# Feed-forward of layer 0: bias rows written into the product banks by ScalarE instead of added by bias matmuls

## The chip, the cores and the metric

The kernel runs on one core of a Trainium2 chip. The metric is device time in microseconds (us), the median of several runs. The engines are named as in the profile: PE is TensorE (PEld its weight loads), ACT is ScalarE, DVE is VectorE, POOL is GpSimd, SP is SyncE. SP here only issues DMAs. A name with a q behind it (PEq, SPq) is an engine's instruction queue.

## What is computed

Two decoder layers in one launch, on 2048 tokens of width 512: attention 0, feed-forward 0, attention 1, feed-forward 1. The change lies in feed-forward 0, of which the reference says (x is the residual stream; the constant names are cut):

```python
def _quant_dequant_fp8(x):                 # per row, per chunk of 128
    scale = maximum(amax(chunk), 1e-4) / 448
    return (chunk / scale).astype(float8_e4m3fn) * scale
D = Xd @ W0d.T + bias0                     # 512 -> 1792
D = gelu(D, approximate=False)
Dd = quant_dequant(D.astype(bfloat16))
E = Dd @ W1d.T + bias1                     # 1792 -> 512
x = x + E.astype(bfloat16)
```

Xd, W0d and W1d are the layer-normed input and the two weights after the same quantisation. The biases bias0 (1792 values) and bias1 (512) are bfloat16.

## The kernel before

Each stage is one function with one block of instructions per engine; a block begins when every engine has ended the one before. `ffn0` works through 16 tiles of 128 tokens. Operands of the products are split into a high and a low float16 part, and a product is the sum of three passes (high by high, high by low, low by high). Products are scaled by 64 (`WEIGHT_SCALE`), and ScalarE divides by 64 where it reads a bank.

**One tile.** The input is quantised (ACT L1083, DVE `quant_x`, POOL L1277), transposed by PE into the bank `xt` (L1035), and split into XD by ACT (`high_x`, L1124) and DVE (`low_x`, L1206). The first product fills four banks `db0` to `db3`, 448 of the 1792 columns each: one bias matmul (L1026) and twelve of the product (L1028). Gelu (ACT L1113) reads each bank into DB. DVE takes the maxima (`amax_d`, L1184), works out scales in fifteen small steps (`scales_d`, L70 to L85), ACT multiplies by the reciprocals (L1093, 14 pieces), DVE rounds to the grid (`grid_d`, L100 to L107, and `off_grid_d`, L1202), ACT multiplies by the scales (L1100), and ACT and DVE split into HL (`high_d`, L1108; `low_d`, L1214). SP transposes HL into DT by DMA (L1005, L1007). The second product goes into the one bank `eb`: one bias matmul (L1041, 512 columns), then 42 of the product (L1045). ACT reads it (`out_e`, L1120) and POOL adds it to X (L1282).

**The bias matmul.** Its stationary operand `ones` is 128 by 128, zero but for a first row of ones; its moving operand `B0S` or `B1S` has the scaled bias in row 0 and zeros in the others. It is the first matmul of each accumulation group (start=True), so it also opens the bank. To have this, SP loads bias0 and bias1 into one partition (L995, L996), POOL clears B0S, B1S and `ones` and sets the row (L1292 to L1295), and DVE scales the biases (`scale_biases`, L1226) in step -1. PE waits for both before its first product (L1057 to L1060).

**Order.** All engines but SP go through the steps -1 to 18 (`steps`, L983); tiles 6 to 13 run in a hardware loop of two tiles a turn. In step i PE does the first product of tile i, the transposes of tile i+1, and the second product of tile i-2 (L1055). ACT does in this order: `out_e` of tile i-3, L1083 for tile i+2, gelu of the first three banks of tile i, the first half of L1100 for tile i-1, gelu of the fourth bank, `high_x` of tile i+1, `high_d` and the second half of L1100 and `high_d` for tile i-1, L1093 for tile i (L1132). DVE: `grid_d` of tile i-1, `quant_x` of i+2, `off_grid_d` of i-1, `amax_d` of i, `low_x` of i+1, `scales_d` of i, `low_d` of i-1 (L1228). So gelu of tile i waits on ACT behind work that itself waits for DVE, and DVE starts tile i's grid only after ACT has done the first seven pieces of L1093. In steps 0 to 4 DVE also has a piece each of the layer norm and scales of the last quarter of X.

**End of the stage.** In step 15 SP loads the key and value weights of attention 1 (L337), and ACT and DVE split them (L1147, L1245). In steps 16 and 17 PE projects keys and values with them into the same banks `db` (L348). Behind step 16 ACT and DVE do two parts of the next layer norm (L189 is ACT's square root in it), so `out_e` of tile 14 stands on ACT behind them, and PE's second product of tile 15 waits for `out_e` of tile 14, since there is one bank `eb`. The memory `SH` that holds the biases becomes the query weights WQ1 in step 17 (L1166).

The weights W0T of the first product are loaded during attention 0 (L748); W1T is loaded by SP behind the biases (L997), on the same queue.

Of the kernel before, what the change touches and what calls it, by code (L numbers as in the profile page):

```python
# [16 lines left out]
BF16 = mybir.dt.bfloat16  # L17
# [6 lines left out]
P = 128  # L24
# [898 lines left out]
def ffn0(nc, sb, pb, sem, X, ident, ahead_of_ffn0, x_scales, x_buffers, x_sems, w1t_dram, b0, b1,  # L923
# [4 lines left out]
    with ExitStack() as ph:  # L928
# [8 lines left out]
        B0, B1, B0S = SH[0:1, 0:INNER], SH[0:1, INNER:INNER + DIM], SH[:, INNER + DIM:2 * INNER + DIM]  # L937
        B1S = sb(ph, "B1S", [P, DIM], BF16)
        ones = sb(ph, "ones0", [P, P], BF16)
# [15 lines left out]
                 "xt_done xt_hi xt_lo d_done ones_done bias_zeroed bias_ready gelu_done da_done dstep dw_done dcut dbits dm_done dsum "  # L955
# [37 lines left out]
        @block.sync  # L993
        def _(sp):
            sp.dma_start(B0[:, :], b0.partition_broadcast(1)).then_inc(S["b_ld"], 16)  # L995
            sp.dma_start(B1[:, :], b1.partition_broadcast(1)).then_inc(S["b_ld"], 16)  # L996
            sp.dma_start(W1T[:, :, :, :], w1t_dram.rearrange("p (s c n) -> p s c n", s=2, c=IC)).then_inc(S["w1_ld"], 16)  # L997

            def step(i):
                hidden = ahead(i, -1)  # L1000
                if live(hidden):
                    if live(ahead(hidden, -1)):
                        sp.wait_ge(S["e_done"], count(hidden, 1, 0))
                    sp.wait_ge(S["dh_done"], count(hidden, 2, 2))
                    sp.dma_start_transpose(DT[:, 0, :, :], HL[:, 0, :, :].rearrange("p c t -> p (c t)")).then_inc(S["dt_done"], 16)  # L1005
                    sp.wait_ge(S["dl_done"], count(hidden, 2, 2))
                    sp.dma_start_transpose(DT[:, 1, :, :], HL[:, 1, :, :].rearrange("p c t -> p (c t)")).then_inc(S["dt_done"], 16)  # L1007

            for i in range(TILES + 1):
                if i == TILES - 1:  # L1010
                    sp.wait_ge(S["xqs_done"], TILES)
                    load_kv1(sp)
                if i == TILES:
                    sp.wait_ge(S["d_done"], 4 * TILES)
                    load_weights1(sp)
                step((0, i))

        @block.tensor
        def _(pe):
            def first_product(i, qs):  # L1020
                for q in qs:
                    if q == 0:
                        pe.wait_ge(S["xt_lo"], count(i, 1, 1))
                    if live(ahead(i, -1)):
                        pe.wait_ge(S["gelu_done"], count(i, 4, q - 3))
                    pe.matmul(db[q][:, 0:NQ], ones[:, :], B0S[:, q * NQ:(q + 1) * NQ], start=True, stop=False)  # L1026
                    for n, (k, (a, b)) in enumerate([(k, ab) for ab in PASSES for k in range(KC)]):
                        last = pe.matmul(db[q][:, 0:NQ], XD[:, i[1] % 2, a, k, :], W0T[:, b, k, q * NQ:(q + 1) * NQ],  # L1028
                                         start=False, stop=n == 3 * KC - 1)
                    last.then_inc(S["d_done"], 1)  # L1030
# [7 lines left out]
            def second_product(i):  # L1038
                if live(ahead(i, -1)):
                    pe.wait_ge(S["eb_done"], count(i, 1, 0))  # L1040
                pe.matmul(eb[:, :], ones[:, :], B1S[:, :], start=True, stop=False)  # L1041
                pe.wait_ge(S["dt_done"], count(i, 32, 32))
                for c in range(IC):
                    for a, b in PASSES:
                        last = pe.matmul(eb[:, :], DT[:, a, c, :], W1T[:, b, c, :],  # L1045
                                         start=False, stop=c == IC - 1 and (a, b) == PASSES[-1])
# [8 lines left out]
            def step(i):  # L1055
                old, nxt = ahead(i, -2), ahead(i, 1)
                if fixed(i) == 0:  # L1057
                    pe.wait_ge(w0_ld, 16)
                    pe.wait_ge(S["ones_done"], 2)
                    pe.wait_ge(S["bias_ready"], 2)  # L1060
# [15 lines left out]
        def _(act):  # L1076
# [38 lines left out]

            def out_e(i):
# [3 lines left out]
                act.activation(EB[:, i[1] % 2, :], eb[:, :], ACT.Copy, scale=UNSCALE).then_inc(S["eb_done"], 1)  # L1120

# [10 lines left out]
            def step(i):  # L1132
# [5 lines left out]
                if fixed(i) == -1:  # L1138
                    high_x(nxt)
# [4 lines left out]
                if fixed(i) == TILES - 1:  # L1144
                    act.wait_ge(loaded1["skv_ld"], 32)
                    act.wait_ge(S["xt_done"], TILES)
                    act.activation(WKV1[:, 0, :, :, :], SKV1[:, :, :, :], ACT.Copy, scale=WEIGHT_SCALE).then_inc(S["kvw_hi"], 1)  # L1147
                if live(hidden):
# [3 lines left out]
                if live(nxt) and fixed(i) != -1:  # L1152
                    high_x(nxt)
                if live(hidden):
# [7 lines left out]
                if fixed(i) == TILES + 1:  # L1162
                    high_keys_values((2, 3))
                    act.wait_ge(loaded1["sq_ld"], 16)
                    for j in range(REP):
# [7 lines left out]
        def _(dve):  # L1173
# [48 lines left out]
            def scale_biases():  # L1222
                dve.wait_ge(S["b_ld"], 32)
                dve.wait_ge(S["bias_zeroed"], 2)
                for scaled, bias in ((B0S, B0), (B1S, B1)):
                    dve.tensor_scalar(scaled[0:1, :], bias[:, :], WEIGHT_SCALE, None, ALU.mult).then_inc(S["bias_ready"], 1)  # L1226

            def step(i):  # L1228
                hidden, nxt, after = (ahead(i, by) for by in (-1, 1, 2))
                if fixed(i) == -1:  # L1230
                    low_x(nxt)
                    scale_biases()
# [39 lines left out]
        def _(pool):  # L1272
# [17 lines left out]

            for zeros in (B0S, B1S):
                pool.memset(zeros[:, :], 0.0).then_inc(S["bias_zeroed"], 1)  # L1292
            pool.memset(ones[:, :], 0.0).then_inc(S["ones_done"], 1)
            pool.wait_ge(S["ones_done"], 1)
            pool.memset(ones[0:1, :], 1.0).then_inc(S["ones_done"], 1)  # L1295
# [746 lines left out]
```

## Time and profile before

| | |
|---|---|
| runs | 1663.59, 1663.84, 1664.19 us; median 1663.84 |
| profiled execution, first to last instruction | 1663.4 us |
| busy share of that span | PE 91%, DVE 77%, ACT 47%, POOL 17% |
| mean granted TensorE clock | 0.968 |
| feed-forward 0 | from 1023.7 to 1380.8 us of the span |

The page gives the span of the profiled execution and no other time for it; the runs shown are 0.2 to 0.8 us longer. All times of rows are us from the start of that span. A matmul's duration in a row reaches until its results are out, so consecutive matmuls overlap: what one costs is the distance between starts, not its duration. Some matmul records are missing in a trace: L1041 shows its 16 weight loads and no matmuls. "Idle before" in a row is the time in which that engine did nothing just before, and the name behind the arrow is what released it.

### The profile page before, as it was taken

The numbers are of one execution on the slowest core, as the hardware profiler recorded it, in microseconds if no ns is written. First come the engines' busy times: TensorE is split into PE (matmuls) and PEld (weight loads), VectorE is DVE, ScalarE is ACT, GpSimd is POOL, SyncE is SP. The second block draws the span as 40 slices with busy tenths as digits, with TensorE's granted clock in tenths as the row PEclk, the third lists the DMA queues.
The fourth block names the chain that finished last, engine by engine and source line by source line (L and its number), as shares of the span: only waits on it lengthen the run. The fifth ranks groups of instructions, "written<-read, shape, count | busy, mean of one in ns | idle before, by whom it ended". The sixth has DMA issues, their size and how long they took to land. (4 is left out here: it accounts for less than half of the span.)

```text
span 1663.4 us, 29998 instructions
## 1 busy us (share of the span) xinstructions
PE 1510.4 (91%) x11382; PEld 803.7 (48%) x11398; DVE 1273.3 (77%) x2386; ACT 789.3 (47%) x1677; POOL 289.0 (17%) x249
## 2 busy tenths in 40 slices
PE   5799999999999999999999987799999998787695
PEld 4455455555555555555555543344444544344353
DVE  6577667667677667767776786899999986999777
ACT  3343433424334243342333332566777763888652
POOL 2001002001011011011011001111211103789620
PEclk7799999999999999999999998899999999899898
DMA  7031231321312212221312112122222350767402
GB/s 265 1 78 51 68 85 26 79 75 43 98 39 66 76 52 64 68 61 52 77 51 62 48 70 102 23 45 45 45 44 44 58 117 1 140 107 123 79 1 101
DMA packets 273838, 113.48 MB, mean 68 GB/s; under 512 B 239154, under 2 KB 255539, under 8 KB 273460
## 3 DMA queue, kind: packets, MB, share of 16 engines
q1 hardware_dynamic: 234820, 78.67, 21.6%
q10 hardware_dynamic: 38896, 33.03, 6.3%
q8 instruction: 94, 1.54, 0.4%
q14 instruction: 28, 0.23, 0.0%
HBM read 44.57 MB, written 11.53 MB: 34 GB/s over the span
## 5 line engine op out<-in xcount | busy, mean ns | idle before, releaser
L627 PE MATMUL xp<-WO,OT 128*128 128x512 f16 x1536 | 341.1, 382 | 5.6 <-DVE X L824 5.6
L585 PE MATMUL pj<-XT,WQ 128*128 128x512 f16 x1536 | 339.0, 381 | 6.4 <-PEq L379 6.4
L627 PEld LDWEIGHTS xp<-WO,OT 128*128 128x128 f16 x1536 | 148.2, 98 | 189.3 <-issue 18.4
L585 PEld LDWEIGHTS pj<-XT,WQ 128*128 128x128 f16 x1536 | 148.4, 98 | 182.3 <-DVE WKV L294 6.7
L705 ACT ACTIVATE E<-E 128x512 f32<-128x512 f32 x64 | 40.1, 627 | 329.0 <-DVE E L801 329.0
L824 DVE SCALAR_TENSOR_TENSOR X<-xp,X 128x512 f32<-128x512 f32 x128 | 88.2, 690 | 113.0 <-PE xp L627 112.0
L565 POOL TENSOR_TENSOR VW<-VW,XB 128x1024 f32<-128x1024 f32 x14 | 32.9, 2351 | 769.8 <-DVE VW L107 769.8
L1028 PE MATMUL db<-W0T,XD 128*128 128x448 f16 x768 | 162.2, 363 | 0.0
L1045 PE MATMUL eb<-W1T,DT 128*128 128x512 f16 x672 | 147.7, 380 | 4.2 <-ACT EB L1120 2.5
L766 DVE SCALAR_TENSOR_TENSOR QT<-pj,QT 128x512 f16<-128x512 f32 x128 | 88.0, 687 | 67.9 <-ACT QT L688 67.6
L1028 PEld LDWEIGHTS db<-W0T,XD 128*128 128x128 f16 x768 | 76.9, 100 | 74.7 <-issue 8.0
L688 ACT ACTIVATE QT<-pj 128x512 f16<-128x512 f32 x128 | 75.5, 590 | 71.1 <-PE pj L585 71.0
L1100 ACT ACTIVATE VD<-VD,dscale 128x128 f32<-128x128 f32 x224 | 68.7, 390 | 75.1 <-DVE VD L1202 75.1
L1045 PEld LDWEIGHTS eb<-W1T,DT 128*128 128x128 f16 x672 | 65.6, 98 | 78.7 <-DMA DT<-HL 1.1
L775 DVE TENSOR_TENSOR OT<-tv,OT 128x512 f16<-128x512 f32 x128 | 82.3, 684 | 13.8 <-ACT OT L697 11.1
L590 PE MATMUL pj<-WKV,CT 128*128 128x128 f16 x1536 | 91.3, 220 | 0.9 <-DVE QT L766 0.9
L585 PE MATMUL pj<-CT,WKV 128*128 128x512 f16 x384 | 88.2, 380 | 4.0 <-DVE QT L766 4.0
L590 PEld LDWEIGHTS pj<-WKV,CT 128*128 128x128 f16 x1536 | 85.9, 98 | 7.7 <-issue 6.3
L697 ACT ACTIVATE OT<-tv 128x512 f16<-128x512 f32 x128 | 69.3, 593 | 26.2 <-PE tv L616 26.2
L710 ACT ACTIVATE EH<-E 128x512 f16<-128x512 f32 x64 | 40.3, 630 | 84.5 <-DVE E L813 84.5
L1401 POOL TENSOR_TENSOR CT<-CT 128x512 f16<-128x512 f32 x64 | 72.6, 1159 | 16.9 <-ACT CT L1631 16.7
L1093 ACT ACTIVATE VD<-DB,drec 128x128 f32<-128x128 bf16 x224 | 67.2, 387 | 12.3 <-DVE drec L85 12.3
(236 smaller groups left out, 2427.0 us busy)
## 6 DMA issues: line engine op xcount, KB each, us to landing
W0T<-in_L_xattn_wq ACTq DMA_DIRECT2D x7, 1024.0 KB, 5.3
W0T<-in_L_xattn_wo ACTq DMA_DIRECT2D x7, 1024.0 KB, 5.0
CS<-in_ctx SPq DMA_DIRECT2D x4, 1024.0 KB, 10.1
X<-in_x SPq DMA_DIRECT2D x4, 1024.0 KB, 11.2
out<-X SPq DMA_DIRECT2D x8, 512.0 KB, 3.6
XB<-in_L_ffn_W ACTq DMA_DIRECT2D x28, 128.0 KB, 2.8
w0t<-XB ACTq DMA_DIRECT2D x7, 512.0 KB, 3.3
w1t<-W0T ACTq DMA_DIRECT2D x7, 512.0 KB, 3.8
```

The lines of the kernel that those rows point to most:

```text
L585: last = pe.matmul(bank[:, :], w, src[:, b, k, tokens], start=n == 0, stop=n == 3 * KC - 1)
L590: last = pe.matmul(bank[:, i * P:(i + 1) * P], CT[:, a, k, own], WKV[:, b, k, 1, :], start=n == 0, stop=n == 3 * KC - 1)
L627: last = pe.matmul(xp[i % 2][:, :], OT[:, a, j, i * P:(i + 1) * P], WO[:, b, j, :], start=n == 0, stop=n == 3 * REP - 1)
L688: act.activation(QT[:, 0, :, u, :], q_bank(u), ACT.Copy, scale=UNSCALE).then_inc(S["pj_hi"], 1)
L697: act.activation(o_out(0, pair, h), o_bank(h), ACT.Copy).then_inc(S["ot_hi"], 1)
L766: dve.scalar_tensor_tensor(out=to[0], in0=q_bank(u), scalar=UNSCALE, in1=to[1], op0=ALU.mult, op1=ALU.subtract).then_inc(S["pj_lo"], 1)
L775: dve.tensor_tensor(o_out(1, pair, h), o_bank(h), o_out(0, pair, h), ALU.subtract).then_inc(S["ot_lo"], 1)
L824: dve.scalar_tensor_tensor(out=xt, in0=xp[i % 2][:, :], scalar=UNSCALE, in1=xt, op0=ALU.mult, op1=ALU.add).then_inc(S["x_acc"], 1)
L1028: last = pe.matmul(db[q][:, 0:NQ], XD[:, i[1] % 2, a, k, :], W0T[:, b, k, q * NQ:(q + 1) * NQ], start=False, stop=n == 3 * KC - 1)
L1045: last = pe.matmul(eb[:, :], DT[:, a, c, :], W1T[:, b, c, :], start=False, stop=c == IC - 1 and (a, b) == PASSES[-1])
L1100: last = act.activation(VD[:, r, c, :], VD[:, r, c, :], ACT.Copy, scale=ds_[:, r, c:c + 1])
L1401: pool.tensor_tensor(EH[:, 1, q, :], E[:, q, :, :].rearrange("p u n -> p (u n)"), EH[:, 0, q, :], ALU.subtract).then_inc(S["e_lo"], 1)
```

## The change

The biases are loaded into all 128 partitions. `ones`, B0S, B1S, POOL's four memsets and DVE's `scale_biases` are gone. In step -1 PE opens each of the five banks once with a matmul whose result nobody reads (`open_banks`), now ahead of the first transposes, and ACT then writes the scaled biases into all five banks, ahead of `high_x` and L1083. From then on all product matmuls have start=False and add to what stands in the bank, and ACT writes the bias anew after each read: into `db0` to `db2` behind the three gelus of a step (for the next tile), into `db3` behind `high_x`, into `eb` behind `out_e`. PE waits for these writes (`bias_set`, `e_bias_set`) where it waited for gelu and `out_e`. ACT waits for its own gelu or `out_e` ahead of the write into the bank that this read, and ahead of L1166 for all its writes.

```diff
-        B0, B1, B0S = SH[0:1, 0:INNER], SH[0:1, INNER:INNER + DIM], SH[:, INNER + DIM:2 * INNER + DIM]
-        B1S = sb(ph, "B1S", [P, DIM], BF16)
-        ones = sb(ph, "ones0", [P, P], BF16)
+        B0, B1 = SH[:, 0:INNER], SH[:, INNER:INNER + DIM]
@@ block.sync
-            sp.dma_start(B0[:, :], b0.partition_broadcast(1)).then_inc(S["b_ld"], 16)
-            sp.dma_start(B1[:, :], b1.partition_broadcast(1)).then_inc(S["b_ld"], 16)
+            sp.dma_start(B0[:, :], b0.partition_broadcast(P)).then_inc(S["b_ld"], 16)
+            sp.dma_start(B1[:, :], b1.partition_broadcast(P)).then_inc(S["b_ld"], 16)
@@ block.tensor
+            def open_banks():
+                for q in range(4):
+                    pe.matmul(db[q][:, 0:NQ], W0T[:, 0, 0, 0:P], W0T[:, 0, 0, 0:NQ], start=True, stop=True).then_inc(S["opened"], 1)
+                pe.matmul(eb[:, :], W0T[:, 0, 0, 0:P], W0T[:, 0, 0, 0:DIM], start=True, stop=True).then_inc(S["opened"], 1)
             def first_product(i, qs):
...
-                    if live(ahead(i, -1)):
-                        pe.wait_ge(S["gelu_done"], count(i, 4, q - 3))
-                    pe.matmul(db[q][:, 0:NQ], ones[:, :], B0S[:, q * NQ:(q + 1) * NQ], start=True, stop=False)
+                    pe.wait_ge(S["bias_set"], count(i, 4, q + 1))
...
             def second_product(i):
-                if live(ahead(i, -1)):
-                    pe.wait_ge(S["eb_done"], count(i, 1, 0))
-                pe.matmul(eb[:, :], ones[:, :], B1S[:, :], start=True, stop=False)
+                pe.wait_ge(S["e_bias_set"], count(i, 1, 1))
                 pe.wait_ge(S["dt_done"], count(i, 32, 32))
...
-                if fixed(i) == 0:
+                if fixed(i) == -1:
                     pe.wait_ge(w0_ld, 16)
-                    pe.wait_ge(S["ones_done"], 2)
-                    pe.wait_ge(S["bias_ready"], 2)
+                    open_banks()
@@ block.scalar
+            def preset_d(qs):
+                for q in qs:
+                    act.activation(db[q][:, 0:NQ], B0[:, q * NQ:(q + 1) * NQ], ACT.Copy, scale=WEIGHT_SCALE).then_inc(S["bias_set"], 1)
+            def preset_after_gelu(i, qs):
+                act.wait_ge(S["gelu_done"], count(i, 4, qs[-1] + 1))
+                preset_d(qs)
+            def preset_e():
+                act.activation(eb[:, :], B1[:, :], ACT.Copy, scale=WEIGHT_SCALE).then_inc(S["e_bias_set"], 1)
             def out_e(i):
...
+                if live(ahead(i, 1)):
+                    act.wait_ge(S["eb_done"], count(i, 1, 1))
+                    preset_e()
...
                 if fixed(i) == -1:
+                    act.wait_ge(S["b_ld"], 32)
+                    act.wait_ge(S["opened"], 5)
+                    preset_d(range(4))
+                    preset_e()
                     high_x(nxt)
                 if live(after):
                     x_times_rec(after)
                 if live(i):
                     gelu(i, (0, 1, 2))
...
+                if live(nxt) and live(i):
+                    preset_after_gelu(i, (0, 1, 2))
                 if live(hidden):
                     d_times_scale(hidden, 0)
                 if live(i):
                     gelu(i, (3,))
                 if live(nxt) and fixed(i) != -1:
                     high_x(nxt)
+                if live(nxt) and live(i):
+                    preset_after_gelu(i, (3,))
...
                     act.wait_ge(loaded1["sq_ld"], 16)
+                    act.wait_ge(S["bias_set"], 4 * TILES)
+                    act.wait_ge(S["e_bias_set"], TILES)
@@ block.vector
-            def scale_biases():
...
@@ block.gpsimd
-            for zeros in (B0S, B1S):
-                pool.memset(zeros[:, :], 0.0).then_inc(S["bias_zeroed"], 1)
-            pool.memset(ones[:, :], 0.0).then_inc(S["ones_done"], 1)
-            pool.wait_ge(S["ones_done"], 1)
-            pool.memset(ones[0:1, :], 1.0).then_inc(S["ones_done"], 1)
```

## Rows read from the trace of the kernel before

**Rows 1.** Busy time by stretch: stretch, length, PE, PEld, DVE, ACT, POOL, PEclk, DMA, GB/s.
```profile
1170.00:1326.00 156.00, 155.58 (x784) 77.82 (x790) 146.71 (x283) 112.94 (x320) 26.94 (x15) 1.00 0.26 47
```
**Rows 2.** Timeline of one tile's turn: start, us, what, [idle before <-releaser].
```profile
1187.29 0.68 DVE L1206 TENSOR_TENSOR XD<-xt,XD 128x512 f16<-128x512 f32 x1
...
1189.87 0.35 PE L1026 MATMUL db<-SH,ones 128*128 128x448 bf16 x1
...
1191.07 4.20 ACT L1093 ACTIVATE VD<-DB,drec 128x128 f32<-128x128 bf16 x14 [0.51 <-DVE drec L85]
...
1192.33 0.35 PE L1026 MATMUL db<-SH,ones 128*128 128x448 bf16 x1
...
1193.25 0.63 DVE L100 TENSOR_SCALAR VD<-VD 128x896 uint32<-128x896 uint32 x1 [0.22 <-ACT VD L1093]
...
1200.36 9.23 PE L1045 MATMUL eb<-W1T,DT 128*128 128x512 f16 x42
...
1209.43 0.35 PE L1026 MATMUL db<-SH,ones 128*128 128x448 bf16 x1
...
1212.76 0.63 DVE L100 TENSOR_SCALAR VD<-VD 128x896 uint32<-128x896 uint32 x1 [0.20 <-ACT VD L1093]
```
**Rows 3.** Waits from 1165 to 1330: who for whom, us in total, times, longest.
```profile
ACT VD L1100 <- DVE VD L1202: 35.9, 8, 4.8
ACT VD L1093 <- DVE drec L85: 4.9, 9, 0.7
...
DVE VD L100 <- ACT VD L1093: 1.9, 9, 0.2
```
**Rows 4.** Timeline: three gelus in a row on ACT.
```profile
1196.82 1.38 ACT L1113 ACTIVATE DB<-db 128x448 bf16<-128x448 f32 x3
```
**Rows 5.** Groups by line: four copies out of SBUF; last columns busy us, mean ns, idle.
```profile
L1166 ACT ACTIVATE SH<-W0T 128x512 f16<-128x512 f32 x4 | 2.2, 637 | 0.0
```
**Rows 6.** Timeline of the start of feed-forward 0.
```profile
1023.68 0.30 SPq L995 DMA_DIRECT2D SH<-in_L_ffn_bias  x1
...
1024.38 0.60 ACT L1124 ACTIVATE XD<-xt 128x512 f16<-128x512 f32 x1 [13.92 <-PE xt L1035]
...
1025.01 0.69 DVE L1206 TENSOR_TENSOR XD<-xt,XD 128x512 f16<-128x512 f32 x1 [1.63 <-ACT XD L1124]
...
1025.83 0.61 DVE L1226 TENSOR_SCALAR SH<-SH 1x1792 bf16<-1x1792 bf16 x1
...
1027.23 0.53 PE L1026 MATMUL db<-SH,ones 128*128 128x448 bf16 x1 [2.88 <-POOL ones L1295]
...
1031.34 0.35 PE L1026 MATMUL db<-SH,ones 128*128 128x448 bf16 x1
```
**Rows 7.** DMA issues of the whole span: size, median us from issue to landing.
```profile
w0t<-XB ACTq DMA_DIRECT2D x7, 512.0 KB, 3.3
...
W0T<-in_L_ffn_bias SPq DMA_DIRECT2D x1, 256.0 KB, 6.8
```
**Rows 8.** Waits of SP's queue from 1300 to 1385: us in total, times, longest.
```profile
SPq L1005 <- PE eb L1045: 6.3, 3, 2.8
```
**Rows 9.** Timeline of the end of feed-forward 0.
```profile
1335.71 1.06 ACT L1147 ACTIVATE VW<-VW 128x1024 f16<-128x1024 f32 x1 [0.84 <-DMA VW<-in_L_xattn_Wv]
...
1339.27 1.09 DVE L1184 TENSOR_REDUCE damax<-DB 128x7 f32<-128x896 bf16 x1 [0.70 <-ACT DB L1113]
...
1368.35 0.21 ACT L189 ACTIVATE root<-var_eps 128x4 f32<-128x4 f32 x1 [4.10 <-DVE var_eps L159]
1368.47 0.58 ACT L1120 ACTIVATE EB<-eb 128x512 bf16<-128x512 f32 x1
...
1369.33 9.23 PE L1045 MATMUL eb<-W1T,DT 128*128 128x512 f16 x42 [2.51 <-ACT EB L1120]
```
**Rows 10.** Timeline: two first matmuls of a tile after idle time of PE.
```profile
1061.03 0.56 PE L1026 MATMUL db<-SH,ones 128*128 128x448 bf16 x1 [9.35 <-DVE XD L1206]
...
1126.97 0.36 PE L1026 MATMUL db<-SH,ones 128*128 128x448 bf16 x1 [1.10 <-DVE XD L1206]
```

More of the change, by code:

```diff
@@ L954, in ffn0 @@
         names = ("w1_ld b_ld kvw_hi kvw_lo qw_hi "
-                 "xt_done xt_hi xt_lo d_done ones_done bias_zeroed bias_ready gelu_done da_done dstep dw_done dcut dbits dm_done dsum "
+                 "xt_done xt_hi xt_lo d_done opened bias_set e_bias_set gelu_done da_done dstep dw_done dcut dbits dm_done dsum "
                  "dq_done dqs_done dh_done dl_done dt_done e_done eb_done x_done")
@@ L1023, in first_product @@
                         pe.wait_ge(S["xt_lo"], count(i, 1, 1))
-                    if live(ahead(i, -1)):
-                        pe.wait_ge(S["gelu_done"], count(i, 4, q - 3))
-                    pe.matmul(db[q][:, 0:NQ], ones[:, :], B0S[:, q * NQ:(q + 1) * NQ], start=True, stop=False)
+                    pe.wait_ge(S["bias_set"], count(i, 4, q + 1))
                     for n, (k, (a, b)) in enumerate([(k, ab) for ab in PASSES for k in range(KC)]):
                         last = pe.matmul(db[q][:, 0:NQ], XD[:, i[1] % 2, a, k, :], W0T[:, b, k, q * NQ:(q + 1) * NQ],
-                                         start=False, stop=n == 3 * KC - 1)
+                                         start=False, stop=n == 3 * KC - 1, skip_group_check=True)
                     last.then_inc(S["d_done"], 1)
@@ L1045, in second_product @@
                         last = pe.matmul(eb[:, :], DT[:, a, c, :], W1T[:, b, c, :],
-                                         start=False, stop=c == IC - 1 and (a, b) == PASSES[-1])
+                                         start=False, stop=c == IC - 1 and (a, b) == PASSES[-1], skip_group_check=True)
                 last.then_inc(S["e_done"], 1)
@@ L1220, in low_keys_values @@
                     low_kv1(dve, db[unit], unit // 2, unit % 2)
-            def scale_biases():
[L1223 to L1226, printed above, removed]
             def step(i):
@@ L1231, in step @@
                     low_x(nxt)
-                    scale_biases()
                 if live(hidden):
```

## The prediction

> **What bounds the kernel now.** I read the busy times of the stretch in which feed-forward 0 runs evenly, then the timeline of one tile's turn, then who waits for whom there, and last the two ends of the stage, where the change adds or moves steps.
>
> In the even stretch, eight tiles long, PE is busy for 155.58 of 156.00 us [rows 1]. That looks like a stage bound by PE, and 80 matmuls fewer like a gain. The timeline says otherwise. PE starts a tile every 1209.43 - 1189.87 = 19.56 us, and DVE its grid every 1212.76 - 1193.25 = 19.51 us [rows 2]: two cycles of nearly one length. Which of them drives? `low_x` has XD ready at 1187.97, and PE takes it up 1.90 us later [rows 2], so PE is behind and nobody is held up by it. DVE's own waits in the stretch are 1.9 us in nine grids, all for ACT's L1093, which waits for DVE's `scales_d` [rows 3]: the ring is DVE, ACT, DVE, with no PE in it. DVE's busy share of 146.71 in 156.00 [rows 1] is not slack; what is missing lies between small dependent steps. ACT waits 4.8 us a tile for DVE ahead of L1100, and about half a microsecond ahead of L1093 [rows 3]. The first is room for new work on ACT, the second hardly any.
>
> So a faster PE only starts each tile sooner after `low_x`, and the time changes where PE or ACT stands in a chain: at the start, in the 0.51 us ahead of L1093, and at the end.
>
> **PE's part.** A quarter of the first product is 13 matmuls in 1192.33 - 1189.87 = 2.46 us [rows 2], 0.189 each; one of 512 columns costs (1209.43 - 1200.36) / 42 = 0.216 [rows 2]. A tile loses 4 x 0.189 + 0.216 = 0.97 us, 16 tiles 15.6 us. In the ring this is worth nothing from tile 2 on; DVE's 1.9 us of waits bounds it from above. Tile 0's first product is an exception, below. Its five opening matmuls run while the biases are still coming, and cost nothing as long as that takes longer than they do: about 1 us at 0.2 each, 2 at half the clock.
>
> **The start.** Now PE's first matmul waits until 1027.23 for POOL's `ones`; `high_x` starts at 1024.38 and `low_x` ends at 1025.70, 1.32 later [rows 6]. After the change `high_x` stands behind five writes of ACT, and these behind the biases.
> - Biases: issued at 1023.68; the one-partition loads had landed when DVE scaled them at 1025.83 [rows 6]. Now 448 and 128 KB. The nearest size, 512 KB, lands in 3.3 us; another broadcast bias of 256 KB took 6.8, queued behind other loads [rows 7]. Scaled by size, 3.3 x 576 / 512 = 3.7: landed at 1027.4, between 1025.8 and 1030.5.
> - Five writes: no row has ACT writing a bank. Three gelus of 448 columns take 1.38 us, 0.46 each [rows 4]; four copies of 512 out of SBUF take 2.2 us, 0.55 each, and 0.64 for one alone [rows 5]. A piece of 128 columns takes 4.20 / 14 = 0.30 [rows 2], which a wider one exceeds. I take 0.47 and 0.55, nearest in size: 4 x 0.47 + 0.55 = 2.4, between 1.5 and 3.2.
> - So XD of tile 0 is ready at 1027.4 + 2.4 + 1.3 = 1031.1 and PE starts at 1031.2, 4.0 later than now. Its four bias matmuls are gone, 0.8 less: gelu, and with it DVE's ring, starts **3.2 us later** (0.7 to 7.1 by the bounds). L1083 of tile 1, also behind the writes, has the whole first product of tile 0 as cover.
>
> The Trainium skill, "ScalarE: Activation LUTs", section "The pipeline for one element", says that ScalarE writes PSUM faster than SBUF. No row here shows it; by it the five writes take less than 2.4 us and the start costs less than 3.2.
>
> **The ring.** Per tile ACT gets 4 x 0.47 + 0.55 = 2.4 us. The writes to `db0` to `db2` stand ahead of the 4.8 us wait [rows 3] and vanish in it; `eb`'s delays L1083 and three gelus by 0.6, in the same cover. The write to `db3` stands ahead of `high_d`, L1100 and so L1093: 0.47 against 0.51 of idle [rows 2]: **0 us**. If a write takes its 0.64, 0.13 a tile for some ten tiles: +1.3. Were that idle gone, every tenth on ACT would be a tenth on DVE. The added waits for ACT's own gelus name work that is just ending; behind them queue `high_d` and L1100, counted here.
>
> **The end.** SP's transposes waited for PE three times, up to 2.8 us [rows 8]. Behind one of them stands the key and value load, for which ACT waits 0.84 us; it delays gelu of tile 15, for which DVE waits 0.70 [rows 9]. PE now comes some 2.8 us earlier, this wait goes, and DVE is late by 0.7 less, not more, since ACT's L1100 stands next: -0.7. Then the last second product: `out_e` of tile 14 stands behind the layer norm's square root on ACT (1368.35) and ends at 1369.05; PE's 42 matmuls start at 1369.33 [rows 9]. Now ACT's write of `eb` comes between, 0.6 us, where the bias matmul took 0.28 with its wait: +0.35. Sum **-0.35** (-0.7 to +0.4).
>
> **The clock at the end.** PE has everything else done earlier and waits longer for this last product: 2.51 us now [rows 9], plus 2.8, less 0.35: about 5.0. After 9.35 us of idle time the first matmul took 0.56 us, after 2.88 us 0.53, after 1.10 us 0.36 [rows 6, 10]: the lower clock level twice, the higher once. But at the end 2.51 us cost no clock: 42 matmuls in 9.23, as in the even stretch [rows 2, 9]. 5.0 is beyond both, so I expect the lower level. Its price: the first quarter at the start took 1031.34 - 1027.23 = 4.11 [rows 6] where 2.46 is usual: **+1.65**. Nothing hides it: `out_e`, POOL's add and the next block follow.
>
> **Sum.** 3.2 + 0 - 0.35 + 1.65 = +4.5 us. The profiled span is 1663.4 and the median of the runs 1663.84, 0.4 more; I add the difference to the median: **1668.3 us**. About 0.2%, 3.3 us, is what a measurement of this kernel can tell from no change.
>
> **Rivals.**
> - The clock stays up for the last product (not slower). What decides is whether 5.0 us of idle time lowers it; for it speaks the row with 2.51, against it those with 2.88 and 9.35. Then +2.85, 1666.7: within 0.2%. Chance 0.27.
> - PE was the bound: its 155.58 of 156.00 us speaks for it, the 1.90 us of lag and DVE's few waits against. Then eight tiles gain 0.97 each, 1668.3 - 7.8 = 1660.5. Chance 0.06.
> - A write into a bank costs 0.64 or more and the ring grows: 1669.6. Chance 0.10.
> - The broadcast loads land late, as the 6.8 us row: +3.1, 1671.4. Chance 0.08.
> - The clock falls in every tile, since PE now idles 19.51 - 18.59 = 0.92 us in each. Then a tile's PE time is 18.59 + 1.65 = 20.2, above the ring by 0.7, for nine tiles +6: 1674. The 1.10 us row speaks against. The Trainium skill, "TensorE: Matmul & The Clock Gate", section "HAM oscillation", describes such a repeated loss in a loop with gaps. Chance 0.04, and 0.45 for my forecast.
>
> **Range and chances.** 1664.5 to 1671.5 takes in the forecast, the kept clock, the longer ring and the late load, and leaves out PE as the bound and the clock in every tile. Slower: 0.40 of the forecast's 0.45, and 0.22 of the last three rivals, 0.62. Faster: 0.06. The rest, 0.32, within 0.2%.
>
> **What would show it.** Right: `low_x` of tile 0 ends near 1031; DVE still waits 0.2 us a tile for L1093 with 19.5 us between grids; PE waits about 0.9 us a tile for XD; the last second product takes some 10.9 us. Wrong: a tile's turn near 18.6 (PE was the bound); L1093 no longer waiting for `drec` and the turn longer (ring); the last product in 9.2 (clock); the ring's start moved by under 2 or over 5 us.

## The result and the profile after

The changed kernel takes 1670.53 us (median of 9 runs, 1668.90 to 1671.27); the kernel before, run beside it, 1664.44. The ratio is 1.0029, with an interval of 1.0020 to 1.0039: **slower by 3.3 to 6.5 us**, 4.8 by the ratio and 6.1 by the medians. The forecast was 1668.3, in a range to 1671.5.

The profiled execution has a span of 1669.0 us. Its feed-forward 0 goes from the first issue at 1022.67 to the next block's first matmul at 1386.35, 363.68 us; before it was 1023.68 to 1380.77, 357.09. What follows took 282.65 and 282.63 us. So **all of it, 6.59 us in these two executions, lies in the stage that was changed** (the stage began 1.0 us sooner; over all the profiles below it begins anywhere from 1020.98 to 1023.92).

The even stretch first: busy times by stretch of the kernel after, columns as in [rows 1].

```profile
1170.00:1326.00 156.00, 150.10 (x755) 73.54 (x753) 146.73 (x278) 133.48 (x361) 27.87 (x16) 1.00 0.25 47
```

PE is busy 5.5 us less, ACT 20.5 us more, DVE as before. The clock stays at 1.00. Waits from 1165 to 1330, columns as in [rows 3]:

```profile
ACT VD L1098 <- DVE VD L1224: 23.0, 9, 2.6
...
PE db L1029 <- DVE XD L1228: 5.9, 8, 1.0
DVE VD L100 <- ACT VD L1091: 1.7, 8, 0.2
...
ACT VD L1091 <- DVE drec L85: 0.4, 1, 0.4
```

Two things changed places. PE now waits for XD, 0.7 to 1.0 us a tile, where it was late before. And ACT's slack is used up: ahead of its scaling (L1098, before L1100) it waits 2.6 us a tile instead of 4.8, and ahead of L1091 (before L1093) no longer. The timeline of one tile shows how exactly:

```profile
1187.84 2.16 ACT L1098 ACTIVATE VD<-VD,dscale 128x128 f32<-128x128 f32 x7 [2.63 <-DVE VD L1224]
...
1190.80 0.53 ACT L1116 ACTIVATE db<-SH 128x448 f32<-128x448 bf16 x1
...
1191.56 0.67 DVE L1228 TENSOR_TENSOR XD<-xt,XD 128x512 f16<-128x512 f32 x1
...
1192.37 9.25 PE L1029 MATMUL db<-W0T,XD 128*128 128x448 f16 x48 [1.00 <-DVE XD L1228]
...
1194.34 0.95 ACT L1106 ACTIVATE HL<-VD 128x896 f16<-128x896 f32 x1
...
1195.13 0.17 DVE L85 TENSOR_TENSOR drec<-dtmp 128x14 f32<-128x14 f32 x1
...
1195.34 4.20 ACT L1091 ACTIVATE VD<-DB,drec 128x128 f32<-128x128 bf16 x14
...
1203.16 1.48 ACT L1116 ACTIVATE db<-SH 128x448 f32<-128x448 bf16 x3
...
1211.80 4.52 PE L1029 MATMUL db<-W0T,XD 128*128 128x448 f16 x23 [0.68 <-DVE XD L1228]
```

ACT ends `high_d` at 1195.29 and DVE ends `drec` at 1195.30: they arrive together. The turn is 1211.80 - 1192.37 = 19.43 us; in both kernels turns of 19.43 and 19.51 alternate. The first instruction of DVE's grid for tiles 0, 14 and 15, before and then after:

```profile
1047.02 0.62 DVE L100 TENSOR_SCALAR VD<-VD 128x896 uint32<-128x896 uint32 x1
...
1327.56 0.63 DVE L100 TENSOR_SCALAR VD<-VD 128x896 uint32<-128x896 uint32 x1 [0.22 <-ACT VD L1093]
...
1345.77 0.63 DVE L100 TENSOR_SCALAR VD<-VD 128x896 uint32<-128x896 uint32 x1 [0.22 <-ACT VD L1093]
```

```profile
1051.16 0.62 DVE L100 TENSOR_SCALAR VD<-VD 128x896 uint32<-128x896 uint32 x1
...
1331.83 0.63 DVE L100 TENSOR_SCALAR VD<-VD 128x896 uint32<-128x896 uint32 x1 [0.22 <-ACT VD L1091]
...
1349.25 0.63 DVE L100 TENSOR_SCALAR VD<-VD 128x896 uint32<-128x896 uint32 x1 [0.22 <-ACT VD L1091]
```

From the first grid to that of tile 14 the ring takes 0.13 us more than before, 280.67 and 280.54; from there to the last grid it takes 17.42 and 18.21.

The start, in the timeline (answers to [rows 6]):

```profile
1022.67 0.36 SPq L993 DMA_DIRECT2D SH<-in_L_ffn_bias  x1
1022.71 0.92 PE L1020 MATMUL db<-W0T 128*128 128x448 f16 x4 [1.06 <-PEq L485]
...
1027.69 1.94 ACT L1116 ACTIVATE db<-SH 128x448 f32<-128x448 bf16 x4 [18.00 <-DMA SH<-in_L_ffn_bias]
1029.58 0.58 ACT L1123 ACTIVATE eb<-SH 128x512 f32<-128x512 bf16 x1
1030.10 0.57 ACT L1136 ACTIVATE XD<-xt 128x512 f16<-128x512 f32 x1
...
1031.45 11.57 PE L1029 MATMUL db<-W0T,XD 128*128 128x448 f16 x48 [7.17 <-DVE XD L1228]
...
1042.86 0.60 PE L1036 MATMUL xt<-ident,VW 128*128 128x128 f32 x4
```

The biases land 5.02 us after the first issue, five writes take 2.41, and PE's first product starts 8.78 us after the issue, where it was 3.55. It then takes 42.86 - 31.45 = 11.41 us, at the lower clock level for nearly its first 5; before, it took 11.49 (1027.23 to 1038.72). So DVE's ring starts 5.15 us later, counted from the start of the stage: 28.49 after it, where it was 23.34.

The end (answers to [rows 9]), and the clock in stretches of the last product:

```profile
1371.83 0.20 ACT L189 ACTIVATE root<-var_eps 128x4 f32<-128x4 f32 x1 [4.10 <-DVE var_eps L159]
1371.94 0.58 ACT L1129 ACTIVATE EB<-eb 128x512 bf16<-128x512 f32 x1
...
1372.55 0.60 ACT L1123 ACTIVATE eb<-SH 128x512 f32<-128x512 bf16 x1
...
1373.21 10.93 PE L1044 MATMUL eb<-W1T,DT 128*128 128x512 f16 x42 [3.63 <-ACT eb L1123]
```

```profile
1373.21:1375.00 1.79, 1.79 (x7) 0.77 (x8) 1.72 (x5) 1.79 (x4) 0.54 (x1) 0.75 0.00 0
1375.00:1377.00 2.00, 2.00 (x6) 0.65 (x5) 2.00 (x4) 1.22 (x3) 0.00 (x0) 0.50 0.00 0
```

The last 42 matmuls take 10.93 us instead of 9.23, with the granted clock at 0.50, the 1.2 GHz level, from 1375 to 1377. From the last grid to the start of this product it takes 0.40 us more, and the last grid itself comes 0.79 us sooner behind that of tile 14. **Sum: 5.15 + 0.13 - 0.79 + 0.40 + 1.70 = 6.59**, what the stage is longer.

### The profile page after: what moved, and what is told of

It reads as the page before. It is cut to its first block and busy times, and to the rows that moved or that the text cites. A ratio compares the mean times of both kernels' runs of the same rounds, so it can differ in the third digit from the quotient of the medians.

```text
span 1669.0 us, 29950 instructions
## 1 busy us (share of the span) xinstructions
PE 1499.0 (90%) x11323; PEld 794.2 (48%) x11323; DVE 1272.0 (76%) x2384; ACT 829.4 (50%) x1757; POOL 285.3 (17%) x245
## 5 line engine op out<-in xcount | busy, mean ns | idle before, releaser
L1029 PE MATMUL db<-W0T,XD 128*128 128x448 f16 x768 | 154.6, 363 | 33.9 <-DVE XD L1228 33.9
L1098 ACT ACTIVATE VD<-VD,dscale 128x128 f32<-128x128 f32 x224 | 68.8, 390 | 50.5 <-DVE VD L1224 50.5
L1292 POOL TENSOR_TENSOR VW<-VW,xscale 128x512 f32<-128x512 f32 x15 | 24.3, 1617 | 281.3 <-DVE VW L1200 273.6
```

The source lines that it names most:

```text
L1098: last = act.activation(VD[:, r, c, :], VD[:, r, c, :], ACT.Copy, scale=ds_[:, r, c:c + 1])
```

## The experiments

Each experiment has one profile and 5 to 12 timed runs. "Stage" is as above; "first product" is its start after the start of the stage; the last column is the duration of the last second product. Ratios are against the kernel before, run beside each; its medians there were 1665.20 to 1665.56, so rows are better compared by their ratios than by their medians.

| kernel | median us | ratio (95%) | stage | first product | last product |
|---|---|---|---|---|---|
| before | 1664.44 | | 357.09 | 3.55 | 9.23 |
| after | 1670.53 | 1.0029 (1.0020 to 1.0039) | 363.68 | 8.78 | 10.93 |
| e1_no_bias_matmuls | 1663.99 | 0.9994 (0.9985 to 1.0003) | 357.52 | 3.55 | 10.93 |
| e2_early_biases | 1666.54 | 1.0015 (1.0005 to 1.0025) | 359.54 | 5.03 | 11.07 |
| e3_x_first | 1668.46 | 1.0024 (1.0014 to 1.0035) | 360.54 | 6.02 | 11.06 |
| e4_write_twice | 1674.70 | 1.0056 (1.0042 to 1.0070) | 367.99 | 9.24 | 10.86 |
| e5_keep_busy | 1671.53 | 1.0034 (1.0021 to 1.0047) | 363.54 | 10.50 | 9.24 |
| e6_out_first | 1666.51 | 1.0013 (1.0003 to 1.0023) | 362.54 | 10.91 | 9.22 |
| e7_all | 1660.59 | 0.9975 (0.9966 to 0.9985) | 354.44 | 3.11 | 9.22 |
| e8_before_out_first | 1662.34 | 0.9990 (0.9980 to 0.9999) | 355.29 | 3.55 | 9.24 |
| e9_hold_w1t | 1668.90 | 1.0023 (1.0013 to 1.0033) | 362.37 | 7.45 | 10.93 |
| e10_own_wait | 1668.90 | 1.0024 (1.0015 to 1.0034) | 362.27 | 7.37 | 10.93 |
| e11_hold_and_busy | 1669.67 | 1.0023 (1.0012 to 1.0034) | 361.58 | 7.91 | 9.24 |
| e12_hold_again | 1668.47 | 1.0023 (1.0014 to 1.0033) | 361.40 | 7.48 | 10.83 |

### e1: what PE's 15.6 us are worth

The kernel before without its 80 bias matmuls; the biases are left out of the result, all else (loads, memsets, waits) stays.

```diff
-                    pe.matmul(db[q][:, 0:NQ], ones[:, :], B0S[:, q * NQ:(q + 1) * NQ], start=True, stop=False)
...
-                                          start=False, stop=n == 3 * KC - 1)
+                                          start=n == 0, stop=n == 3 * KC - 1)
...
-                pe.matmul(eb[:, :], ones[:, :], B1S[:, :], start=True, stop=False)
...
```

> The kernel before without its 80 bias matmuls (the first matmul of each product opens the bank); the biases are left out of the result, nothing else changes. Theory (the ring DVE, ACT, DVE sets the pace, PE has slack): 15.6 us less on PE give almost nothing. First product of tile 0 -0.8, end of the stage -0.8 and -0.25, and up to +1.7 if the clock falls ahead of the last product: between -1.9 and +0.2 us against the kernel before, and about 19.5 us between DVE's grids. Rival (PE is the bound of the even stretch): 0.97 us for each of 8 or more tiles, 8 to 15 us faster, about 18.6 us between the grids.

The time is that of the kernel before within its interval, and the stage is 0.43 us longer in the profile. From the first grid to that of tile 14 it takes 280.63 us, before 280.54. Busy times by stretch, and two waits from 1165 to 1330:

```profile
1170.00:1326.00 156.00, 152.43 (x769) 75.14 (x768) 146.77 (x278) 113.20 (x325) 26.96 (x15) 1.00 0.27 50
```

```profile
ACT VD L1091 <- DVE drec L85: 5.0, 9, 0.7
PE db L1027 <- DVE XD L1204: 3.6, 5, 0.8
```

PE gets idle time and gives none of it to the ring: **PE did not bound the stage**. ACT's half microsecond ahead of its L1091 is still there (5.0 us, before 4.9 [rows 3]), so it is the writes that use it up. The last product, after 2.81 us of idle time, took 10.93: the clock can be lost there without any write, by the saving on PE alone.

### e2 and e3: the start

e2 loads the biases during attention 0, into memory that its query weights have left by then. e3 leaves the loads and puts `high_x` and L1081 ahead of the wait for the biases.

```diff
+            sp.wait_ge(S["pj_done"], GROUPS * SPG * 6)
+            sp.dma_start(SH[:, 0:INNER], b0.partition_broadcast(P)).then_inc(bias_ld, 16)
+            sp.dma_start(SH[:, INNER:INNER + DIM], b1.partition_broadcast(P)).then_inc(bias_ld, 16)
```

```diff
                 if fixed(i) == -1:
+                    high_x(nxt)
+                if live(after):
+                    x_times_rec(after)
+                if fixed(i) == -1:
                     act.wait_ge(S["b_ld"], 32)
...
-                    high_x(nxt)
-                if live(after):
-                    x_times_rec(after)
```

> The kernel after, with the biases loaded by SP during attention 0 into the same memory, once the last projection has read it; the order on ACT as in the kernel after. Theory (the first product waits for the biases to land, 5.0 us after their issue, then for five writes): ACT starts to write when the banks are open, some 1.5 us after the block's start instead of 5.0; the first product starts 3.5 us earlier, perhaps 0.5 more by a shorter low clock: 3.5 to 4.2 us faster than the kernel after, about +1 to +2 against the kernel before. Rival (the start is covered by other work, and the loss lies in the ring or at the end): within 0.5 us of the kernel after.

> The kernel after, with high_x and L1081 of step -1 ahead of the wait for the biases and the five writes on ACT. Theory (landing, writes and the split of x stand in one chain): the first product then starts with the first bank's write, 0.5 us after the landing, instead of after five writes, high_x and low_x: 3.2 us earlier, so 3.2 us faster than the kernel after, +1.5 to +2.5 against the kernel before. Rival (landing alone sets the start): no more than 0.5 us faster than the kernel after.

With the loads out of the way the first product starts 3.75 us sooner than in the changed kernel and the stage is 4.14 shorter; with `high_x` first 2.76 and 3.14. Neither reaches the kernel before: the end is as slow as in the changed kernel (11.07 and 11.06). In the timed runs less of the gain shows than the 3.5 to 4.2 and 3.2 us expected: by the ratios e2 is 2.3 us under the changed kernel and e3 0.8, with intervals that overlap the changed kernel's, so for e3 a gain in time is not shown, only the shorter stage.

### e4: is there room for more on ACT?

The write into `db3` is done twice, the second after the first.

```diff
-                    preset_after_gelu(i, (3,))
+                    act.wait_ge(S["gelu_done"], count(i, 4, 4))
+                    act.activation(db[3][:, 0:NQ], B0[:, 3 * NQ:4 * NQ], ACT.Copy, scale=WEIGHT_SCALE).then_inc(S["first_write"], 1)
+                    act.wait_ge(S["first_write"], count(i, 1, 1))
+                    preset_d((3,))
```

> The kernel after, with the write of db3 in steps 0 to 14 done twice. Theory (ACT's half microsecond ahead of L1091 is used up to the last tenth by the one write): a second write delays L1091 and so DVE's grid by its whole 0.45 to 0.55 us in the ten or so tiles where no other work of DVE stands between: 4.5 to 5.5 us slower than the kernel after, about 19.95 us between grids. Rival (ACT still has room there, or PE sets the pace): 0 to 1 us.

From 1165 to 1330 DVE waits 0.6 us a tile for ACT's scaling, where it waited 0.2:

```profile
DVE VD L100 <- ACT VD L1091: 4.5, 8, 0.6
```

A turn is 19.85 us instead of 19.47 on average; the 15 turns together take 4.15 us more, and the stage is 4.31 longer, a little less than the 4.5 to 5.5 expected. So the first write into `db3` just fitted, and of a second, 0.57 with its wait, 0.38 a tile are on the path.

### e5, e11: the clock at the end

16 spare matmuls on PE ahead of the last second product, in e5 alone, in e11 together with e9's edit; e12 is e9's kernel again, run beside e11.

```diff
+                if fixed(i) == TILES - 1:
+                    pe.wait_ge(S["xt_lo"], TILES)
+                    for n in range(WARM):
+                        pe.matmul(xt[:, :], W1T[:, 0, 0, 0:P], W1T[:, 0, 0, :], start=True, stop=True)
```

> The changed kernel, with 16 spare matmuls of 512 columns on PE, into the bank xt that nobody uses any more, ahead of the last second product (about 16 x 0.216 = 3.5 us of work put into its wait). Theory (the lower clock level follows from the idle time ahead of it): less than 2 us of idle time are left ahead of the last second product, it takes 9.2 us instead of 10.9, and the time is about 1.7 us under the changed kernel's, some 3 us over the kernel before. Rival (the low level there has another cause, or something else sets the end of the stage): the last product still takes 10.9, or the time stays within 0.5 us of the changed kernel's.

> The kernel whose load of W1T waits for the biases, and with it the 16 spare matmuls ahead of the last second product. Why again: with the spare matmuls alone the last second product came back to 9.24 us, but the biases had landed 1.7 us later in that profile than in the changed kernel's, and the time did not fall. Here the landing is steadier. Theory (the clock at the end costs 1.7 us, whatever the start does): last second product 9.2 us, and the median about 1.7 us under that of the kernel with the held load alone, run beside it. Rival (something else takes the 1.7 us back): medians within 0.7 us of each other.

> The kernel whose load of W1T waits for the biases, once more, as the control of the run beside it. Both theories: biases landed 3.6 to 4.1 us after the first issue, first product about 7.5 us after the start of the stage, last second product 10.9 us, median near 1668.9.

The last products of e5, e11 and e12 in their timelines:

```profile
1373.06 9.24 PE L1049 MATMUL eb<-W1T,DT 128*128 128x512 f16 x42 [1.60 <-ACT eb L1128]
```

```profile
1372.38 9.24 PE L1050 MATMUL eb<-W1T,DT 128*128 128x512 f16 x42 [0.17 <-ACT eb L1129]
```

```profile
1371.89 10.83 PE L1045 MATMUL eb<-W1T,DT 128*128 128x512 f16 x42 [5.35 <-ACT eb L1124]
```

The first half of the theory holds: with little idle time ahead, the product is back at 9.24, and from the last grid to the end the stage is 1.68 us shorter in e5 than in the changed kernel, 1.59 in e11 than in e12. The second half, that the time falls by as much, **was not seen in either**: the medians are no lower (1671.53 against the changed kernel's 1670.53; 1669.67 beside e12's 1668.47). The ratios of e11 and e12 are equal, 1.0023, but each is known only to about 0.0011, 1.8 us, either way. The profiles show two places where it went. The first ring started later in both (1.4 us than the changed kernel's in e5, where the biases landed late; 1.8 than e12's in e11, landing and a longer low clock), which is some 340 us ahead of the edit's place and so not its doing. And what follows the stage, the same code in all, took 285.3 and 284.3 us, where it took 281.6 to 283.3 in all the others. In e11 the loss lies near the end of attention 1; busy times of a stretch there, e12 and then e11, at equal distance from the end of the stage:

```profile
1569.00:1581.00 12.00, 7.67 (x48) 3.13 (x48) 7.81 (x25) 3.42 (x7) 4.40 (x4) 0.86 0.14 26
```

```profile
1568.00:1580.00 12.00, 8.05 (x41) 3.03 (x42) 7.86 (x25) 3.81 (x7) 4.75 (x4) 0.65 0.17 33
```

The clock, 0.86 in one, is 0.65 in the other, under the same sparse work. Whether the higher clock level at the end of one stage brings this about or these two profiles met it by chance stays open; the kernels e6 to e8 have the same higher level there and 282.6 to 283.3 behind it.

### e6, e8: who holds up the last product

`out_e` of tile 14 (and in e6 the write of `eb` behind it) moved ahead of the layer norm's square roots; e8 does so in the kernel before.

```diff
-                if live(older):
+                if live(older) and fixed(i) != TILES + 1:
                     out_e(older)
...
+                if fixed(i) == TILES:
+                    out_e(ahead(i, -2))
                 if fixed(i) in LN_STEPS:
```

> The changed kernel, with ACT's out_e of tile 14 and the write of eb behind it moved ahead of the layer norm's square roots. Theory (the last second product waits only because out_e of tile 14 stands behind ACT's square root, which waits for DVE): the last second product starts about 3 us sooner, as soon as tile 15 is in DT, with under 2.5 us of idle time ahead of it, so also at the higher clock level: 3 + 1.7 less what DVE's layer norm then holds up, about 3.5 to 4 us under the changed kernel, near 1667. Rival (DT of tile 15 or the layer norm gates the end anyway): less than 0.5 us.

> The kernel before, with ACT's out_e of tile 14 alone moved ahead of the layer norm's square roots. Control for the run that has all three moves. Theory: the last second product of the kernel before also waits for this out_e (2.51 us), which at the higher level either way is worth 1.2 to 1.8 us. If the move brings 3 us or more here, the gain of the three moves together owes nothing to ACT's bias writes. Rival: under 0.5 us.

The last product of e6 and of e8:

```profile
1373.31 9.22 PE L1044 MATMUL eb<-W1T,DT 128*128 128x512 f16 x42 [1.45 <-DMA DT<-HL]
```

```profile
1365.29 9.24 PE L1045 MATMUL eb<-W1T,DT 128*128 128x512 f16 x42 [0.79 <-DMA DT<-HL]
```

Both now wait for DT alone, and not long. From the last grid to the end, e6 is 3.91 us shorter than the changed kernel and e8 1.83 shorter than the kernel before, as expected. By the ratios e6 is 2.7 us under the changed kernel (4.0 by the medians, which were not run beside each other); e8's ratio stands for 0.2 to 3.3 us under the kernel before. So the place of `out_e` behind the square root was a cost already before; the change added the write and the clock to it.

### e9, e10: why the biases land late

e9 lets SP issue the load of W1T only once both biases have landed. e10 gives bias1 a semaphore of its own and writes `eb` behind `high_x` and L1081.

```diff
+            sp.wait_ge(S["b_ld"], 32)
             sp.dma_start(W1T[:, :, :, :], w1t_dram.rearrange("p (s c n) -> p s c n", s=2, c=IC)).then_inc(S["w1_ld"], 16)
```

```diff
-                    act.wait_ge(S["b_ld"], 32)
+                    act.wait_ge(S["b_ld"], 16)
                     act.wait_ge(S["opened"], 5)
                     preset_d(range(4))
-                    preset_e()
...
+                if fixed(i) == -1:
+                    act.wait_ge(S["b1_ld"], 16)
+                    preset_e()
```

> The changed kernel, in which SP issues the load of W1T (3584 KB) only after both bias loads have landed. In five profiles so far the 448 KB of bias0 landed 3.5 to 3.8 us after their own issue, the 128 KB of bias1 4.6 to 6.7 us after theirs. Theory (the small load is late because W1T's packets, issued right behind it, share the DMA engines with it): both have landed some 4.0 to 4.4 us after the first issue (128 KB more at the rate of the first 448), where it was 5.0 to 7.1, and the first product starts 7.7 to 8.2 us after the start of the stage, where it was 8.8 to 10.9; DVE's ring starts sooner by as much, the rest is the same. Rival (a broadcast load of this size is late by itself): 128 KB still land 4.6 us or more after their issue.

> The changed kernel, with a wait of its own for bias1: ACT writes the four banks db as soon as bias0 has landed, then does high_x and L1081, and only then waits for bias1 and writes eb, which the second product needs two steps later. Theory (bias0 lands 3.5 to 3.8 us after its issue, bias1 is what is late): writes start at about 3.7, first product 6.8 to 7.0 us after the start of the stage, where it was 8.8 to 10.9: stage about 1.9 us shorter than the changed kernel's in its profile, 361.8 of 363.7. Rival (ACT's start is gated by the opening matmuls or by something else than bias1): first product later than 8.2 us.

DMA issues from 1015 to 1045, size and us from issue to landing, first of the changed kernel, then of e9:

```profile
W1T<-w1t SPq DMA_DIRECT2D x1, 3584.0 KB, 13.9
SH<-in_L_ffn_bias SPq DMA_DIRECT2D x1, 448.0 KB, 3.6
SH<-in_L_ffn_bias SPq DMA_DIRECT2D x1, 128.0 KB, 4.6
```

```profile
W1T<-w1t SPq DMA_DIRECT2D x1, 3584.0 KB, 12.9
SH<-in_L_ffn_bias SPq DMA_DIRECT2D x1, 448.0 KB, 3.1
SH<-in_L_ffn_bias SPq DMA_DIRECT2D x1, 128.0 KB, 3.3
```

Alone, both have landed 3.7 us after the first issue (1021.51 to 1025.20), and the first product starts at 7.45, sooner even than expected. In six profiles with W1T right behind, the 128 KB took 4.6 to 6.7 us, and the writes started up to 7.15 us after the first issue. **What is late is the small last load, and the cause is the 3584 KB behind it**, issued 0.47 us later on the same queue. The Trainium skill, "DMA: Bandwidth & Descriptors", section "Queues, rings and completion order", says that each DMA engine takes the descriptors of a ring in order but that a later one may finish its write before an earlier one. No row here shows the order of single writes, and the loads as wholes landed in the order of their issue; what the rows show is that a place ahead in the queue did not keep the small load from being late. e10 confirms it from the other side (first product at 7.37), though bias0 took 4.1 us there, so the 6.8 to 7.0 expected was missed. The edits take 1.3 and 1.4 us from the stage in these profiles, e9's 2.3 in e12.

### e7: all moves together

e2's loads and e6's `out_e`, and at the start only the write of `db0` ahead of `high_x`, the others behind it.

```diff
                     act.wait_ge(S["opened"], 5)
-                    preset_d(range(4))
-                    preset_e()
+                    preset_d((0,))
                     high_x(nxt)
+                    preset_d((1, 2, 3))
+                    preset_e()
```

> The changed kernel with three moves at once: biases loaded during attention 0; at the start only the write of db0 ahead of high_x, the other four writes behind it and ahead of L1081; and out_e of tile 14 with the write of eb ahead of the layer norm's square roots. Theory (the change costs only at the start and the end, the ring is untouched): first product about 3.1 us after the start of the stage, 3.55 before the change; last second product at the higher level and some 3 us sooner; the stage about 353.7 us long, where it was 357.1 before the change and 363.7 after: about 3 us under the kernel before (ratio 0.998). Rival (the writes cost in the ring as well, and the start is not all of it): not under the kernel before.

Its first and its last product:

```profile
1024.12 9.25 PE L1031 MATMUL db<-W0T,XD 128*128 128x448 f16 x48 [1.50 <-DVE XD L1233]
```

```profile
1363.62 9.22 PE L1046 MATMUL eb<-W1T,DT 128*128 128x512 f16 x42 [1.06 <-DMA DT<-HL]
```

Both at the higher clock level, after 1.50 and 1.06 us of idle time. 1660.59 us, ratio 0.9975: **this version beats both kernels**. The control e8 has 0.9990 without any write of a bias, so a good part of the gain is the place of `out_e`. What the bias writes themselves bring, 354.44 against 355.29 us in the profiles, lies within the intervals of the two ratios, and isn't shown.

## Why the prediction was right, and where its terms were off

The forecast was +4.5 us; the ratio says +4.8, the medians +6.1, the two profiles +6.59. Against the profiles the miss is the start; the other terms come within 0.15.

**What bounds the stage.** Right: DVE's ring with ACT, not PE. e1 takes PE's work away without a gain, and e4 adds 0.57 us to ACT and lengthens the turn by 0.38. But it was closer than the prediction took it to be: before the change PE's lag behind `low_x` grows from 1.94 us at tile 7 (1168.38 to 1170.32) to 2.42 at tile 14 (1304.78 to 1307.20), so PE was slower than the ring by 0.07 us a tile, and it held the ring up at the last tile (see the end, below).

**The start, +3.2, was the term that was mis-sized: it measured 5.15.** Two of its steps failed.
- "Scaled by size, 3.3 x 576 / 512 = 3.7": it was 5.02, +1.3. The scaling itself was good, since e9 measured 3.7; the step left out the load of W1T that SP issues behind the biases on the same queue. The broadcast row of 6.8 us, which the prediction put down to loads ahead of it, might have been a warning; no run here tells what made that load late.
- "Its four bias matmuls are gone, 0.8 less": the first product got only 0.08 shorter. At 0.189 us a matmul it has 9.07 us of work where it had 9.83, so the lower clock level cost it 2.34 us where it had cost 1.66; the forecast took that cost to be the same. It varies without any change: the first product takes 11.49 us before the change and 12.23 in e8, the same code after the same 2.88 us of idle time, and 11.35 in e9 and 10.45 in e12, one kernel, after 5.85 and 5.86. So these 0.7 us may be chance of the two profiles.
- The rest held: five writes 2.41 (2.4 predicted), from the landing to the first product 3.76 (3.8).

The Trainium skill, "ScalarE: Activation LUTs", states in the section "Step-by-step: what each stage is for", not in the one that the prediction names, that ScalarE writes PSUM faster than SBUF. By that rule the five writes would have taken less than 2.4. The rows show little of it: one write of 512 columns into a bank takes 0.58 to 0.60 us, one copy of 512 within SBUF, of other types, 0.64 [rows 5].

**The ring, 0.** Right, 0.13 over 14 turns, and with nothing to spare: behind the write to `db3` ACT goes on 0.46 us later (1190.80 to 1191.26), and of the 0.51 of idle time ahead of its scaling nothing is left.

**The end, -0.35.** -0.39 measured, -0.79 and +0.40, but the first of these came out in part by luck. ACT's wait for the key and value weights did not vanish, it is 1.75 us now; what vanished is DVE's 0.70 behind it. And it vanishes without the change too: from the grid of tile 14 to that of tile 15 the profile of the kernel before takes 18.21 us, all others 17.41 or 17.42, e8 among them, in which PE has all its bias matmuls:

```profile
1326.78 0.63 DVE L100 TENSOR_SCALAR VD<-VD 128x896 uint32<-128x896 uint32 x1 [0.22 <-ACT VD L1093]
...
1344.19 0.63 DVE L100 TENSOR_SCALAR VD<-VD 128x896 uint32<-128x896 uint32 x1 [0.22 <-ACT VD L1093]
```

The two profiles differ at tile 6. PE's first matmul of it and the busy times of a stretch behind it, before and then e8:

```profile
1149.07 0.36 PE L1026 MATMUL db<-SH,ones 128*128 128x448 bf16 x1 [2.37 <-DVE XD L1206]
```

```profile
1151.00:1153.00 2.00, 2.00 (x7) 0.79 (x6) 1.86 (x7) 1.48 (x5) 0.00 (x0) 0.50 0.13 28
```

```profile
1148.24 0.36 PE L1026 MATMUL db<-SH,ones 128*128 128x448 bf16 x1 [2.38 <-DVE XD L1208]
```

```profile
1150.00:1152.00 2.00, 2.00 (x12) 1.03 (x11) 1.83 (x7) 1.49 (x4) 0.00 (x0) 1.00 0.01 2
```

In the one the clock fell to 0.50, and at tiles 7 to 14 PE was 1.9 to 2.4 us behind `low_x`; in the other it stayed at 1.00, and PE was 0.2 to 0.7 behind. So the lag of 1.90 us that the prediction read as the usual state of PE, and the 0.7 us that it hoped to gain at the end, go back to a clock that was lost in one profile and kept in the other.

**The clock at the end, +1.65.** 1.70 measured. The idle time was 3.63 us and not 5.0, since the product ahead of it, of tile 14, was itself at the lower level (10.91 us); where it was not, as in e2, e3 and e12, the idle time was 5.3. e5 and e11 show that the higher level is back when that idle time is filled with work. They also show that taking this term away did not lower the total in two runs, so 1.7 us is a price of the stage, not surely one of the kernel.

**Rivals.** PE as the bound: e1 rules it out. The clock falling in every tile: PE idles 0.68 to 1.00 us in each tile and its clock is 1.00 through the whole stretch, so not with gaps of this length. The Trainium skill, "TensorE: Matmul & The Clock Gate", section "HAM oscillation", describes such a loss, repeated in a loop with gaps; the even stretch here does not show it. A write of 0.64: it took 0.53. The late load did come, by 1.3 us of the 3.1 it was priced at, up to 3.45 in other profiles.

## What to carry to other kernels

Before counting the work that leaves an engine, find out whether anybody waits for that engine: 15.6 us less on PE were worth nothing, while two loads and five small writes put ahead of the first tile cost 5 us once. A load that something waits for should not have a large load issued right behind it on the queue, even though that one is later in order. TensorE may do its last piece of work at the lower clock level when it gets more idle time ahead of it (1.7 us here), so look there when work is taken off it. And a lag or a wait read from one profile may be the mark of one lost clock: a second profile of the same code would have shown it.

## What was not expected of the hardware

**A later load delays an earlier one**: 128 KB took 3.3 to 3.7 us alone and 4.6 to 6.7 with 3584 KB issued 0.47 us behind it.

**The length of the idle time alone does not tell the clock.** The second product of tile 14, of e12 and then of e11, which ran beside it:

```profile
1352.05 9.22 PE L1045 MATMUL eb<-W1T,DT 128*128 128x512 f16 x42 [2.08 <-DMA DT<-HL]
```

```profile
1352.57 10.91 PE L1050 MATMUL eb<-W1T,DT 128*128 128x512 f16 x42 [2.12 <-DMA DT<-HL]
```

The same work after nearly the same idle time, and 1.7 us between them; tile 6 of the kernel before and of e8, shown above, is another such pair. Of the first products of tiles 0 and 1 and the second ones of tiles 14 and 15 in all these profiles, those after 2.81 us or more took longer, as at the lower level, those after 1.92 or less did not, and between 2.00 and 2.53 it went either way.
